# Attention pairs of a fused attention and expert kernel: q and k projected once and doubled by DMA, values one unit later, shared weights rounded behind the first pair

## Chip, cores and metric

One of the eight cores of a Trainium2 chip. The metric is the device time of one execution in microseconds. The engines are TensorE (PE), VectorE (DVE), ScalarE (ACT), GpSimd (POOL) and SyncE (SP); they run their own instruction streams and meet by semaphores. SP, ACT and POOL can issue DMAs.

## What is computed

```python
# B=16, S=128, D=256, 16 heads of 16; then a feed-forward with a shared and 12 routed experts
q = (layernorm(x) @ Wq.T + bq); k = ctx @ Wk.T + bk; v = ctx @ Wv.T + bv     # split into 16 heads
att = einsum('bhsd,bhtd->bhst', q, k) / sqrt(16)
att = where(pad_mask == 0, -1e9, att); att = where(subsq_mask == 0, -1e9, att)
x = x + einsum('bhst,bhtd->bhsd', softmax(att), v)
xf = layernorm(x)
w = top-2 of (xf @ Wr + br) / 1.5, softmax over the two
x = x + geglu(xf @ Ws1 + bs1) @ Ws2 + bs2 + sum over the two experts of w * (geglu(xf @ We1 + be1) @ We2 + be2)
```

## The kernel before

**Pairs and units.** The 16 batches go through the attention in 8 pairs, each pair in four units: batch `b = n // 2` of the pair, half `u = n % 2` of the heads. A unit makes scores of 8 heads in PSUM `ps_s` (`scores`), DVE takes the maximum and subtracts it (`softmax_shift`, L1011 and L1017, into `prob`), ACT takes the exponential (`exp`, L775), PE transposes the probabilities in two halves through the one bank `ps_t[0]` (`prob_transposes`, L493), ACT copies each half to `probT` (`prob_copy`, L766), PE multiplies with the values (`values`, L505), and after two units ACT copies the output to `outT` (`out_copy`, L771) and PE transposes it (`out_transposes`, L514). DVE divides by the sums (`norm`), adds to x and takes the statistics of the second layernorm (`residual`), and after POOL's square root (`rstd`) applies it (`ln2_apply`).

**One unit behind.** In unit U of the loops PE does the scores of U, and then the transposes and values of unit U-1; between them stand the steps of `PLAN`, which project the next pair: transposes of ctx (`cT`) and of the normed x (`xT`), the k projection in two steps (`k0`, `k1`), v, and q in two steps, and for the pair before the router's transposes and logits (`r`, `l`). All is done in about twice f32r precision: ACT rounds to a high part, DVE takes the difference as the low part, and products are made of high and low parts. Each step passes PE, ACT, DVE in turn; `xb_ready`, `xb_hi` and `xb_free` count them, and the steps take turns on two PSUM banks.

**Doubled heads.** A head has 16 numbers, but scores are products over 32 rows: q's high parts stand in 16 rows and its low parts in the other 16, against k twice. So that PSUM holds this layout at once, the weights of q and k come to the chip with each head's columns twice (`heads` in `kernel`), 512 columns instead of 256, in four groups of 128. `q_st` is what the products read, `q_cut` the high part masked to the low rows, `k_hi` and `k_lo` the parts of k.

**What sets the order.** Each engine's function writes its instructions in program order; `pair(p, par, first, last)` is written once per engine, and pairs 1 to 4 run in hardware loops. POOL before the pairs rounds the shared expert's weights (`convert`, six pieces of 512 columns to high and low) and starts the loads of expert 0. In the pairs it only takes square roots. SP loads ctx, and stores the normed x of the pair before (`save_xn2`).

## Time and profile before

| | us |
|---|---|
| median of 3 runs | 782.37 (781.30 to 784.15) |
| profiled execution | 781.65 |
| its span, first to last instruction | 779.5 |
| PE busy in the span | 640.2 (82%) |
| DVE, ACT, POOL busy | 457.8, 270.1, 330.0 |
| mean granted clock of TensorE | 0.926 of full speed |

The profile is of one execution. The span leaves out 2.15 us of the execution's time. A busy matmul is pipelined with its neighbours, so start-to-start distances tell its cost better than its duration. An engine's idle time before an instruction is given in brackets in a timeline, with the one that released it.

### The profile page before, as it was taken

How to read it: one execution, taken by the hardware profiler on the slowest of the kernel's cores; microseconds unless marked ns; L12 is line 12 of the kernel's file. 1: busy time of each engine (PE TensorE's matmuls, PEld its weight loads, DVE VectorE, ACT ScalarE, POOL GpSimd, SP SyncE). 2: the span in 40 equal slices, each digit the busy share in tenths (PEclk: the TensorE clock that was granted, in tenths of full speed). 3: DMA queues.
4: the chain of work that ended last, by engine and by line, in shares of the span. 5: the costliest groups of instructions: out<-in, count | busy, mean ns of one | idle time of the engine just before them, and what ended most of it. 6: DMA issues, size and time to landing. Idle time of an engine off the chain costs nothing.

```text
span 779.5 us, 16006 instructions
## 1 busy us (share of the span) xinstructions
PE 640.2 (82%) x4977; PEld 590.3 (76%) x4978; DVE 457.8 (59%) x893; ACT 270.1 (35%) x556; POOL 330.0 (42%) x389
## 2 busy tenths in 40 slices
PE   4699899899987776079999999999999999997041
PEld 4577777777865665079999999999999999997041
DVE  4656677676765583056665656656566565663136
ACT  3245555555544311024333333333333333331010
POOL 0610000000000477790847957677878582006710
PEclk9689999999999898579999999999999999999556
DMA  9930101001001143252344435525554241013412
GB/s 305 371 133 15 42 28 40 13 27 42 1 29 41 42 148 109 101 189 61 104 162 150 161 119 191 161 76 193 189 177 153 101 135 40 27 40 99 118 48 81
DMA packets 44289, 83.03 MB, mean 107 GB/s; under 512 B 4832, under 2 KB 32736, under 8 KB 44128
## 3 DMA queue, kind: packets, MB, share of 16 engines
q0 software_dynamic: 11120, 48.24, 18.4%
q1 hardware_dynamic: 32560, 34.04, 13.2%
q10 hardware_dynamic: 576, 0.30, 0.2%
q8 instruction: 21, 0.34, 0.2%
q14 instruction: 12, 0.10, 0.0%
HBM read 60.81 MB, written 19.66 MB: 103 GB/s over the span
## 4 chain that ended last, share of the span: by engine, by line
PE 71%; DVE 8%; another core or an unknown queue 8%; issue 5%; ACT 5%; SPq 1%; DMA 1%; POOL 0%; DVEq 0%; ACTq 0%
PE ps_s L583 27%; PE ps_o L623 15%; PE ps_t L596 5%; PE ps_t L493 4%; PE ps_s L481 4%; PE ps_o L505 4%; PE ps_t L440 3%; ACT probT L766 2%; PE ps_x L440 2%; PE ps_s L476 2%; DVE x_all L1264 2%; PE ps_x L605 1%; DMA br<-in_br 1%; DVE ag L1176 1%
## 5 line engine op out<-in xcount | busy, mean ns | idle before, releaser
L583 PE MATMUL ps_s<-ring,xTh 128*128 (+1 forms) x944 | 203.0, 337 | 4.9 <-issue 4.4
L623 PE MATMUL ps_o<-ring,hTh 128*128 (+1 forms) x644 | 127.3, 297 | 65.6 <-DVE hTl L1188 59.0
L583 PEld LDWEIGHTS ps_s<-ring,xTh 128*128 128x128 f32 x944 | 155.3, 193 | 8.3 <-issue 5.4
L623 PEld LDWEIGHTS ps_o<-ring,hTh 128*128 128x128 f32 x644 | 103.1, 198 | 67.4 <-issue 57.3
L1298 POOL TENSOR_TENSOR ring<-stage,ring 128x512 fp32r<-128x512 f32 x120 | 150.9, 1287 | 2.3
L1176 DVE TENSOR_TENSOR ag<-ps_s,up_bias 128x768 f32<-128x768 f32 (+1 forms) x96 | 88.8, 925 | 67.0 <-PE ps_s L583 45.4
L838 ACT ACTIVATE hTh<-ps_t 128x384 fp32r<-128x384 f32 (+1 forms) x118 | 54.6, 462 | 207.1 <-PE ps_t L596 138.9
L583 PE MATMUL ps_s<-ring,xTl 128*128 (+1 forms) x472 | 115.5, 325 | 2.1 <-issue 2.0
L1286 POOL TENSOR_TENSOR ve<-mv,eps 128x2 f32<-128x2 f32 x16 | 3.1, 197 | 232.4 <-DVE mv L1043 170.9
L623 PE MATMUL ps_o<-ring,hTl 128*128 (+1 forms) x322 | 93.3, 290 | 0.0
L831 ACT ACTIVATE ps_s<-ag 128x384 f32<-128x384 f32 (+1 forms) x118 | 55.1, 467 | 90.7 <-DVE ag L1176 85.4
L583 PEld LDWEIGHTS ps_s<-ring,xTl 128*128 128x128 f32 x472 | 83.8, 192 | 0.6 <-issue 0.6
L1182 DVE TENSOR_TENSOR ag<-ag,ps_s 128x384 f32<-128x384 f32 (+1 forms) x118 | 61.1, 518 | 37.6 <-ACT ps_s L831 31.1
L1188 DVE TENSOR_TENSOR hTl<-ps_t,hTh 128x384 fp32r<-128x384 f32 (+1 forms) x118 | 60.9, 517 | 23.6 <-ACT hTh L838 19.1
L1294 POOL TENSOR_SCALAR ring<-stage 128x512 fp32r<-128x512 f32 x120 | 71.7, 626 | 4.8 <-DVE logits L966 4.0
L596 PE MATMUL ps_t<-const,ag 128*128 128x128 f32 x322 | 57.1, 282 | 8.3 <-issue 7.5
L623 PEld LDWEIGHTS ps_o<-ring,hTl 128*128 128x128 f32 x322 | 63.8, 198 | 0.0
L766 ACT ACTIVATE probT<-ps_t 128x512 f32<-128x512 f32 x64 | 38.2, 596 | 69.5 <-PE ps_t L493 69.5
L1409 POOL DMA_INDIRECT gath<-rows_out,idx_top x32 | 30.8, 961 | 67.1 <-DMA rows_out<-y_row 57.6
L1193 DVE TENSOR_TENSOR xTl<-ps_x,xTh 128x256 fp32r<-128x256 f32 x59 | 25.0, 424 | 50.9 <-ACT xTh L845 44.5
L596 PEld LDWEIGHTS ps_t<-const,ag 128*128 128x128 f32 x322 | 38.5, 143 | 15.0 <-issue 10.4
L1011 DVE TENSOR_REDUCE nmax<-ps_s 128x8 f32<-128x1024 f32 x32 | 39.0, 1220 | 16.6 <-PE ps_s L481 16.5
(194 smaller groups left out, 1018.6 us busy)
## 6 DMA issues: line engine op xcount, KB each, us to landing
stage<-in_w POOLq DMA_DIRECT2D x12, 1536.0 KB, 6.7
stage<-in_w POOLq DMA_DIRECT2D x12, 768.0 KB, 5.4
up_bias<-in_bias POOLq DMA_DIRECT2D x12, 768.0 KB, 4.8
rows_in<-y_row SPq DMA_DIRECT2D x1, 5504.0 KB, 22.3
xrow<-rows_in SPq DMA_DIRECT2D x43, 128.0 KB
rows_out<-y_row SPq DMA_DIRECT2D x43, 128.0 KB, 1.7
cbuf<-in_ctx SPq DMA_DIRECT2D x8, 256.0 KB, 3.2
xn_all<-xn2p SPq DMA_DIRECT2D x8, 256.0 KB, 2.4
```

The costliest lines, as they stand in the source:

```text
L583: last = pe_.matmul(out, x[:, c, :], weights(place, a, half_w), start=n == 0, stop=n == 5)
L596: last = pe_.transpose(ps_t[:, u, c * P:(c + 1) * P], ag[u][:, 0, c * P:(c + 1) * P], ident)
L623: pe_.matmul(ps_o[:, 0:D], h[u][:, c, :], weights(place, a, D), start=n == 0, stop=False)
L766: act.activation(probT[:, jj, :, :], ps_t[:, 0, :].rearrange("p (g t) -> p g t", g=4), ACT.Identity).then_inc(pt_copied, 1)
L831: act.activation(ps_s[:, 2 * u + 1, 0:half_w], ag[u][:, 1, 0:half_w], ACT.Gelu).then_inc(gelu_done[u], 1)
L838: act.activation(hTh[u][:, 0:nch, :], ps_t[:, u, 0:nch * P].rearrange("p (c n) -> p c n", c=nch), ACT.Identity).then_inc(ht_hi[u], 1)
L1011: vec.tensor_reduce(nmax[:, :, :], src, AX.X, ALU.max, negate=True).then_inc(maxed, 1)
L1176: vec.tensor_tensor(ag[u][:, :, 0:half_w], ps_s[:, 2 * u:2 * u + 2, 0:half_w], bias, ALU.add)\
L1182: vec.tensor_tensor(ag[u][:, 0, 0:half_w], ag[u][:, 0, 0:half_w], ps_s[:, 2 * u + 1, 0:half_w], ALU.mult)\
L1188: vec.tensor_tensor(hTl[u][:, 0:nch, :], ps_t[:, u, 0:nch * P].rearrange("p (c n) -> p c n", c=nch), hTh[u][:, 0:nch, :].bitcast(f32), ALU ...
L1294: last = pool.tensor_scalar(hi_ap[:, c:c + PIECE], src[:, c:c + PIECE], 1.0, 0.0, ALU.mult, ALU.add)
L1298: last = pool.tensor_tensor(lo_ap[:, c:c + PIECE], src[:, c:c + PIECE], hi_ap[:, c:c + PIECE].bitcast(f32), ALU.subtract)
```

## The change

1. `wq`, `wk` come with their 256 columns once. The q and k projections are one step each (`PLAN`), of two groups of 128 columns. ACT and DVE write high and low parts into `q_cut` and `k_cut`.
2. These are stored to DRAM (`q_dram` by SP, `k_dram` by POOL), and read back so that q's high and low rows interleave (four DMAs of 128 KB on SP, `spread_q`) and each k row stands twice (eight DMAs of 128 KB on POOL, `spread_k`). PE waits for all of them (`k_in`, `q_in`) before the first scores of a pair.
3. `probT` becomes two buffers, and `values` of unit U-2 stand between the two transposes of unit U-1. `out_transposes`, `norm` and `residual` move with them by a unit. ACT's exponential moves ahead of the output copy and the second probability copy.
4. POOL's rounding of the shared weights and the first loads of expert 0 move behind pair 0; in the prologue q comes before v, and DVE's masks behind v's low part.

```diff
-    PLAN = [["cT", "xT", "k0"], ["v", "k1"], ["r", "q0"], ["q1", "l"]]
+    PLAN = [["cT", "xT", "k"], ["q"], ["v"], ["r", "l"]]
@@ sync @@
+            def save_q(pp, idx):
+                sp.wait_ge(xb_free, idx + 1)
+                sp.dma_start(q_dram.rearrange("(a p) n -> p a n", p=P),
+                             q_cut[:, :, :, :].rearrange("p h g n -> p (h g) n").bitcast(f32)).then_inc(q_saved, 16)
+            def spread_q(pp, par):
+                sp.wait_ge(q_saved, pp * 16 + 16)
+                for g in range(4):
+                    sp.dma_start(q_st[par][:, g, :].bitcast(f32),
+                                 q_dram.rearrange("(h r) n -> r h n", h=2)[g * 64:(g + 1) * 64]).then_inc(q_in, 16)
@@ sync @@
             def pair(p, par, first, last):
                 if not last:
                     sp.wait_ge(xb_ready, index_of("cT", p, first, last) + 1)
-                    load_ctx(p + 2)
+                    if not (isinstance(p, int) and p + 2 >= PAIRS):
+                        load_ctx(p + 2)
+                    save_q(p + 1, index_of("q", p, first, last))
                 if not first:
                     save_xn2(p - 1)
+                if not last:
+                    spread_q(p + 1, 1 - par)
@@ tensor, in pair @@
                     if n == 0:
                         pe.wait_ge(xb_free, before(p, 0, 0, first, last))
+                        pe.wait_ge(k_in, p * 128 + 128)
+                        pe.wait_ge(q_in, p * 64 + 64)
                     scores(p, par, n)
...
                     if prev:
-                        prob_transposes(p * 4 + n - 1, pn, 0)
+                        prob_transposes(p * 4 + n - 1, (n - 1) % 4, 0)
                     next_step()
+                    if behind:
+                        values(p * 4 + n - 2, pn, ppar, pbatch)
                     if prev:
-                        prob_transposes(p * 4 + n - 1, pn, 1)
+                        prob_transposes(p * 4 + n - 1, (n - 1) % 4, 1)
                     next_step()
-                    if prev:
-                        values(p * 4 + n - 1, pn, ppar, pbatch)
                     next_step()
-                    if n % 2 == 0 and prev:
+                    if n % 2 == 1 and behind:
                         out_transposes(pbatch)
@@ scalar, in pair @@
                     if prev:
-                        prob_copy(U, 0)
+                        prob_copy(U, (n - 1) % 4, 0)
                     next_step()
+                    exp(p * 4 + n, n)
+                    if n % 2 == 1 and not (first and n < 2):
+                        out_copy(p * 2 + (n - 2) // 2)
                     if prev:
-                        prob_copy(U, 1)
-                    if n == 0:
-                        next_step()
-                    if n % 2 == 0 and prev:
-                        out_copy(p * 2 + (n - 1) // 2)
-                    exp(p * 4 + n, n)
+                        prob_copy(U, (n - 1) % 4, 1)
@@ vector, in pair @@
-                    if n == 3:
-                        residual(p, 0)
-                    if n == 1 and not first:
+                    if n == 0 and not first:
+                        residual(p - 1, 0)
+                    if n == 2 and not first:
                         residual(p - 1, 1)
@@ gpsimd @@
+            def save_k(pp, idx):
+                if not (isinstance(pp, int) and pp == 0):
+                    gp.wait_ge(ticked, pp * 2)
+                gp.wait_ge(xb_free, idx + 1)
+                pool.tensor_tensor(ptick[:, :], half[:, 0:1], half[:, 0:1], ALU.add).then_inc(ticked, 1)
+                gp.dma_start(k_dram.rearrange("(a p) n -> p a n", p=P),
+                             k_cut[:, :, :, :].rearrange("p h g n -> p (h g) n").bitcast(f32)).then_inc(k_saved, 16)
+            def spread_k(pp, par):
+                gp.wait_ge(ticked, pp * 2 + 1)
+                gp.wait_ge(k_saved, pp * 16 + 16)
+                pool.tensor_tensor(ptick[:, :], half[:, 0:1], half[:, 0:1], ALU.add).then_inc(ticked, 1)
+                for hl, t in ((0, k_hi), (1, k_lo)):
+                    for g in range(4):
+                        rows = k_dram[hl * D + g * 64:hl * D + (g + 1) * 64, :]
+                        gp.dma_start(t[par][:, g, :].bitcast(f32), rows.rearrange("(r o) n -> r o n", o=1)
+                                     .broadcast_to([64, 2, 256])).then_inc(k_in, 16)
...
             def pair(p, par, first, last):
+                if not last:
+                    save_k(p + 1, index_of("k", p, first, last))
                 if not first:
                     rstd(ln2_var, ln2_rs, mv2, ve2, rs2, p - 1, pstep2)
+                if not last:
+                    spread_k(p + 1, 1 - par)
                 if not last and not (isinstance(p, int) and p + 2 >= PAIRS):
                     rstd(ln1_var, ln1_rs, mv1, ve1, rs1, p + 2, pstep)
```

POOL in a pair of the loop, before: `ve`, `rs` with 73 and 74 are the square root of the second layernorm, with 69 and 70 that of the first.

```order
L1286 TENSOR_TENSOR ve_73<-mv_72,eps 128x2
L1288 TENSOR_TENSOR rs_74<-ve_73,half 128x2
L1285 REGISTER_ALU
L1286 TENSOR_TENSOR ve_69<-mv_68,eps 128x2
L1288 TENSOR_TENSOR rs_70<-ve_69,half 128x2
```

The same place now:

```order
L1329 TENSOR_TENSOR ptick<-half 128x1
L1330 DMA k_dram<-k_cut 128x4x256
L1307 TENSOR_TENSOR ve_73<-mv_72,eps 128x2
L1309 TENSOR_TENSOR rs_74<-ve_73,half 128x2
L1335 REGISTER_ALU
L1336 ISA
L1337 TENSOR_TENSOR ptick<-half 128x1
L1341 DMA k_hi_114<-k_dram 128x1x256 x4
L1341 DMA k_lo_116<-k_dram 128x1x256 x4
L1306 REGISTER_ALU
L1307 TENSOR_TENSOR ve_69<-mv_68,eps 128x2
L1309 TENSOR_TENSOR rs_70<-ve_69,half 128x2
```

The store of k stands ahead of the second layernorm's square root of the pair before, the eight reads behind it and ahead of the first layernorm's.

ACT in units 0 and 1 of a loop pair, before:

```order
L766 ACTIVATE probT<-ps_t 128x512
L741 REGISTER_ALU
L743 ACTIVATE aTh_106<-ps_t 128x512
L770 ISA
L771 ACTIVATE outT<-ps_o 128x512
L774 REGISTER_ALU
L775 ACTIVATE prob_118<-prob_118 128x1024
L741 REGISTER_ALU
L754 ACTIVATE k_hi_112<-ps_x,bks 128x256 x2
```

And now, from the exponential of unit 0 to k's high part, and the end of unit 1:

```order
L803 ACTIVATE prob_120<-prob_120 128x1024
L791 REGISTER_ALU
L794 ACTIVATE probT_123<-ps_t 128x512
L770 REGISTER_ALU
L772 ACTIVATE aTh_106<-ps_t 128x512
L770 REGISTER_ALU
L777 ISA
L779 ACTIVATE k_cut<-ps_x,bks 128x256 x2
```

```order
L803 ACTIVATE prob_121<-prob_121 128x1024
L798 ISA
L799 ACTIVATE outT<-ps_o 128x512
L791 REGISTER_ALU
L794 ACTIVATE probT_122<-ps_t 128x512
```

The exponential stood behind the second probability copy, x's high part and the output copy; it now stands ahead of all three.

## Rows read from the trace of the kernel before

**Rows 1.** Timeline: first mask products of pairs 0, 1, 3, 7 (start, us, engine, line, operation).
```profile
30.34 1.01 PE L476 MATMUL ps_s<-mask_b,ident_b 128*128 128x512 bf16 x2 [4.34 <-DVE q_st L955]
...
62.34 0.61 PE L476 MATMUL ps_s<-mask_b,ident_b 128*128 x2
...
118.10 0.60 PE L476 MATMUL ps_s<-mask_b,ident_b 128*128 x2 [0.30 <-DVE logits L966]
...
228.79 0.61 PE L476 MATMUL ps_s<-mask_b,ident_b 128*128 128x512 bf16 x2
```

**Rows 2.** Stretches: length, busy PE, PEld, DVE, ACT, POOL (instructions), clock, DMA share, GB/s.
```profile
62.34:228.79 166.45, 153.40 (x1550) 129.49 (x1549) 115.16 (x240) 90.58 (x156) 9.73 (x22) 1.00 0.08 28
...
49.10:53.18 4.08, 2.20 (x27) 1.64 (x25) 1.56 (x6) 2.69 (x5) 0.90 (x2) 0.99 0.01 4
53.40:59.90 6.50, 6.50 (x36) 5.61 (x35) 4.67 (x9) 0.85 (x3) 0.00 (x0) 0.50 0.00 0
```

**Rows 3.** PE's waits in 62.34 to 228.79: total us, times, longest.
```profile
PE ps_o L514 <- ACT outT L771: 4.4, 6, 0.7
PE ps_t L493 <- ACT probT L766: 4.0, 12, 0.3
```

**Rows 4.** Timeline of the loop pair that begins at 118.10.
```profile
119.78 1.22 DVE L1011 TENSOR_REDUCE nmax<-ps_s 128x8 f32<-128x1024 f32 x1 [1.29 <-PE ps_s L481]
...
120.44 0.60 ACT L766 ACTIVATE probT<-ps_t 128x512 f32<-128x512 f32 x1 [2.82 <-PE ps_t L493]
...
122.16 1.22 DVE L1017 TENSOR_TENSOR prob<-ps_s,nmax 128x1024 f32<-128x1024 f32 x1
...
124.06 1.05 ACT L775 ACTIVATE prob<-prob 128x1024 f32<-128x1024 f32 x1
...
125.17 0.84 ACT L754 ACTIVATE k_hi<-ps_x,bks 128x256 fp32r<-128x256 f32 x2
...
129.94 0.41 DVE L1035 TENSOR_TENSOR x_all<-x_all,att 128x256 f32 x1
...
131.46 0.69 POOL L1288 TENSOR_TENSOR rs<-ve,half 128x2 f32<-128x2 f32 x1
...
141.34 0.48 PE L440 MATMUL ps_t<-aTh,wqh 128*128 128x256 f32 x2
...
142.85 0.60 PE L493 MATMUL ps_t<-const,prob 128*128 128x128 f32 x4
```

**Rows 5.** Timeline of POOL: issues of DMAs.
```profile
330.11 0.96 POOL L1376 DMA_INDIRECT rows_in<-xn_all,idx_top  x1 [0.30 <-issue]
331.07 1.17 POOL L1336 DMA_DIRECT2D up_bias<-in_bias  x2
...
350.45 0.92 POOL L1318 DMA_DIRECT2D stage<-in_w  x1 [0.30 <-POOL ring L1298]
```

**Rows 6.** DMA issues by line: count, KB each, median us from issue to landing.
```profile
stage<-in_w POOLq DMA_DIRECT2D x12, 1536.0 KB, 6.7
...
rows_out<-y_row SPq DMA_DIRECT2D x43, 128.0 KB, 1.7
...
wk_raw<-in_wk SPq DMA_DIRECT2D x1, 512.0 KB, 5.6
...
up_bias<-in_bias POOLq DMA_DIRECT2D x1, 512.0 KB, 4.2
```

**Rows 7.** Timeline of DVE in the prologue.
```profile
13.73 0.88 DVE L958 SCALAR_TENSOR_TENSOR k_lo<-ps_x,bks,k_hi 128x256 fp32r<-128x256 f32 x2 [3.44 <-ACT k_hi L754]
...
18.46 1.23 DVE L985 TENSOR_SCALAR keep<-pad_b 128x2048 f32<-128x2048 int32 x1 [1.98 <-DMA br<-in_br]
...
22.19 1.23 DVE L993 TENSOR_SCALAR mask_b<-keep 128x2048 bf16<-128x2048 f32 x1
```

**Rows 8.** Timeline of PE behind the last pair.
```profile
252.63 0.66 PE L493 MATMUL ps_t<-const,prob 128*128 128x128 f32 x4
...
257.92 0.60 PE L514 MATMUL ps_o<-const,outT 128*128 128x128 f32 x4
```

More of the change, by code:

```diff
@@ L39 @@
 C_ID, C_UP = 0, P
-C_LOQ = 2 * P
-C_LOB = C_LOQ + 1
+C_LOB = 2 * P
 C_ROW = C_LOB + 1
@@ L142, in build @@
     aTl = [put(f"aTl{i}", [P, KC, 256], f32r, low) for i in range(2)]
+    k_cut = put("k_cut", [P, 2, 2, 256], f32r, low)
+    q_cut = put("q_cut", [P, 2, 2, 256], f32r, low)
     q_st = [put(f"q_st{i}", [P, 4, 256], f32r, low) for i in range(2)]
@@ L277, in before @@
     def before(p, n, k, first, last):
-        base = len(PROJ) if first else 9 * p + 5
+        base = len(PROJ) if first else PAIR_STEPS * p + len(PROJ) - 2
         return base + sum(len(steps(m, first, last)) for m in range(n)) + k
@@ L327, in load_ctx @@
                              .rearrange("(t p) d -> p t d", p=P)).then_inc(ctx_in, 16)
+            def save_q(pp, idx):
[7 more added lines that the diff above has]
+                                 q_dram.rearrange("(h r) n -> r h n", h=2)[g * 64:(g + 1) * 64]).then_inc(q_in, 16)
             sp.wait_ge(xb_ready, PROJ.index("cT") + 1)
             load_ctx(1)
+            save_q(0, PROJ.index("q"))
+            spread_q(0, 0)
             sp.wait_ge(w_ready, 3)
@@ L369, in _ @@
             pair(PAIRS - 3, 1, False, False)
-            save_xn2(PAIRS - 3)
+            pair(PAIRS - 2, 0, False, False)
             save_xn2(PAIRS - 2)
@@ L455, in router @@
             def router(s, q, idx, bank):
-                pe.wait_ge(xb_free, idx - (0 if isinstance(idx, int) and idx == PAIR_STEPS_END + 1 else 1))
+                pe.wait_ge(xb_free, idx - (1 if s == "r" else 0))
                 ps = step_bank[bank]
@@ L540, in pair @@
                     prev = not (first and n == 0)
-                    pn, ppar, pbatch = (n - 1) % 4, par if n else 1 - par, p * 2 + (n - 1) // 2
+                    behind = not (first and n < 2)
+                    pn, ppar, pbatch = (n - 2) % 4, par if n >= 2 else 1 - par, p * 2 + (n - 2) // 2
                     def next_step():
@@ L674, in _ @@
             x_transposes(0, 0, 0)
+            values(UNITS - 2, 2, 1, B - 1)
             prob_transposes(UNITS - 1, 3, 1)
-            values(UNITS - 1, 3, 1, B - 1)
             pe.wait_ge(converted, 1)
@@ L679, in _ @@
             up(0, 0, 0, False, SH)
+            values(UNITS - 1, 3, 1, B - 1)
+            up(0, 0, 1, False, SH)
             out_transposes(B - 1)
-            up(0, 0, 1, False, SH)
             router("r", PAIRS - 1, PAIR_STEPS_END, 0)
@@ L757, in step @@
                     sc.wait_ge(xb_free, idx)
+                    if not (isinstance(pp, int) and pp < 2):
+                        sc.wait_ge(pv_done, pp * 8 - 8)
                     act.activation(v_sb[par][:, :, :, 0:HD],
@@ L1068, in pair @@
                     softmax_shift(p * 4 + n, n, next_step if n == 0 and todo else None)
-                    if n == 3:
-                        residual(p, 0)
-                    if n == 1 and not first:
+                    further = not last and not (isinstance(p, int) and p + 2 >= PAIRS)
+                    if n == 0 and not first:
+                        residual(p - 1, 0)
+                    if n == 2 and not first:
                         residual(p - 1, 1)
-                    further = not last and not (isinstance(p, int) and p + 2 >= PAIRS)
-                    if n == 1 and not first:
-                        ln2_apply(p - 1)
                     if n == 2 and further:
                         ln1_stats(p + 2)
-                    if n == 2:
-                        norm(p, 0)
                     while todo:
                         next_step()
-                    if n == 0 and not first:
+                    if n == 2 and not first:
+                        ln2_apply(p - 1)
+                    if n == 3:
+                        norm(p, 0)
+                    if n == 1 and not first:
                         norm(p - 1, 1)
@@ L1221, in tile @@
                     y_copy(t - 1, s - 1 if prev_s is None else prev_s, prev_routed, par, turn)
+            residual(PAIRS - 1, 0)
             x_lo(0)
@@ L1302, in _ @@
             gp.wait_ge(setup_ready, 1)
+            def save_k(pp, idx):
+                if not (isinstance(pp, int) and pp == 0):
+                    gp.wait_ge(ticked, pp * 2)
[12 more added lines that the diff above has]
+                                     .broadcast_to([64, 2, 256])).then_inc(k_in, 16)
             rstd(ln1_var, ln1_rs, mv1, ve1, rs1, 0, pstep)
+            save_k(0, PROJ.index("k"))
+            spread_k(0, 0)
             rstd(ln1_var, ln1_rs, mv1, ve1, rs1, 1, pstep)
-            gp.wait_ge(shared_in, 32)
             SH, PIECE = RING - 1, 512
-            convert(stage1[:, 0:W1S], ring[:, SH, 0:W1S], ring[:, SH, W1S:2 * W1S], 1)
-            convert(stage2[:, 0:W2S], ring[:, SH, 2 * W1S:2 * W1S + W2S],
-                    ring[:, SH, 2 * W1S + W2S:2 * W1S + 2 * W2S], 2).then_inc(converted, 1)
             def load_raw1(e):
```

132 lines of the change are left out of this document (68 added, 64 removed).

## The prediction

> **What bounds the kernel now.** I read the timeline of TensorE (PE) first. It cuts the profiled execution (span 779.5 us, 781.65 us with the 2.15 us around it, 0.7 us under the median of 782.37) into a prologue up to 30.34, attention pair 0 up to 62.34, pairs 1 to 6 up to 228.79, and the last pair up to about 252.6 [rows 1]. Everything behind (feed-forward) is unchanged, and its first steps hang on the last pair, so attention time passes to the end one for one. The change touches only what lies before 262.
>
> In pairs 1 to 6 a pair takes 166.45 / 6 = 27.74 us, PE is busy 153.40 of 166.45 us and its granted clock is 1.00 [rows 2]. The other 13.05 us, 2.2 per pair, are short waits, most of them for ScalarE (ACT): 4.4 us for its copy of the output, 4.0 for its copy of the transposed probabilities [rows 3]. So PE's own work bounds these pairs, 25.6 us each.
>
> **What leaves PE.** A projection step of twelve products of 128x256 takes 141.34 to 142.85, 1.51 us [rows 4]. There are four for q and k per pair, two stay: 3.0 us less. DVE and ACT each lose four of their eight operations for q and k. With the values one unit later, PE no longer waits for the second probability copy. PE's work falls to 25.6 - 3.0 = 22.6 us. If this alone counted, six pairs would give back up to 6 x (27.74 - 22.6) = 31 us. I do not believe it, because of two orders.
>
> **The order inside a pair.** I lay one new pair from its first mask product (0), with durations and gaps of rows. Scores take PE to 1.57; DVE's maximum starts at 1.68 (119.78 against 118.10), the shift at 4.06 and ends at 5.28 (122.16 + 1.22), in a pair whose cT low half sits between, as here [rows 1, 4]. The exponential of 1.05 ends at 6.4 [rows 4], and ACT's order now is exponential, second probability copy, xT high half, k high half (0.6, 0.6, 0.84): k's high half ends at 8.1. DVE's k low half (0.88, [rows 7]) ends at 9.0. Only then is DVE free for the maximum of unit 1, whose scores PE had ready at 7.6. Its shift ends at 11.5, exponential at 12.6, output copy (now behind the exponential) at 13.1: PE, which has run out of work at 11.1, waits 2.0 us for it and starts unit 2 at 13.6. There the shift ends at 17.8 and residual(p-1, 1) starts; its x_all row to the end of the POOL square root is 129.94 to 131.46 + 0.69, 2.2 us [rows 4], so ln2's rs is there at 20.0. Unit 3 waits 1.1 us for the output copy in the same way and ends at 25.5. So with all data at hand a pair is 25.5, not 22.6.
>
> **The order on POOL, where the change hangs.** The eight DMAs that spread k for the next pair stand on POOL behind rstd(ln2, p-1), and so behind the residual in unit 2. They start at 20.1. PE waits for them before the first scores of the next pair (k_in). Two plain issues in a row take 1.17 us, 0.59 each, for 128 rows; one of 768 rows takes 0.92; an indirect one of 128 rows 0.96 + 0.30 [rows 5]. I take 0.59, the row with as many rows and no index list; 0.9 and 1.26 stay as bounds. The last is issued at 20.1 + 7 x 0.59 = 24.3. Landing: a POOL load of 1536 KB takes 6.7 us from its issue and one of 512 KB 4.2 [rows 6], 2.5 us per MB, so 128 KB take about 3.3; a 128 KB store of SP lands in 1.7, the low bound. The last lands at 27.6, PE's next pair begins at about 28.0 with 0.3 to 0.4 for the 2 MB (k 1, q 0.5, xn2 0.5) that share this stretch. q on SP waits for save_xn2(p-1) likewise: xn2 is ready at 20.9, two saves, four issues of 0.5, so it lands near 26.3, behind k's cover. **Bound without a clock effect: 28.0 per pair, +0.3.**
>
> The Trainium skill's page DMA: Bandwidth & Descriptors (Anatomy of one DMA, SWDGE path) gives 2.0 us fixed plus bytes at 436 GB/s for a DMA from POOL; that would be an estimate of 2.3 us for 128 KB. By it a pair would be 1.0 us shorter and the sum 6 us less. The rows of this case speak against it: 512 KB would be 3.2 by the page and took 4.2 [rows 6].
>
> **The clock.** In that order PE idles from 24.0 to 25.1, transposes for 0.45, and idles again from 25.5 to 28.0: busy 0.45 of 4 us. In pair 0 of the trace PE is busy 2.20 of 4.08 us in 49.10 to 53.18, and the clock then stands at 0.50 of its full 2.4 GHz, 1.2 GHz, for the 6.50 us from 53.40 [rows 2]. So I expect a fall at each pair's start. Cold, unit 0's scores take 2.9 instead of 1.57, transposes 0.8 for 0.5; moved through the chain above, k's high half waits for a k step that ends 2.6 later, of which 0.7 lies in slack: k low half at 10.9 instead of 9.0. Everything behind, the residual in unit 2 and the spread too, moves by 1.9. **A pair takes 28.0 + 1.9 = 29.9 us, +2.16 each, +13.0 for six.** If PE falls a second time in the 2.0 us wait of unit 1, the scores of unit 2 come 1.3 later, 31.2.
>
> **Prologue.** Before, DVE ends k's low half at 14.6 and builds the masks from 18.46 (released by the br load) to 23.4 [rows 7]; PE's first scores wait to 30.34 for the last q half [rows 1]. After, weights are half as wide, but POOL does save_k (0.9 + about 3.5 landing), eight issues (4.7), and only then rstd(ln1, 1), for which DVE waits before wvl and the masks: k low half 13.9, saved 18.5, issued 23.8, ln1 rs 24.8, xn 25.6, wvl 26.3, masks of 5.0 us to 31.3. First scores at 31.4: +1.1; if the save lands as slowly as the wk load of 512 KB did (5.6, [rows 6]), +3.
>
> **Pair 0.** It was 32.0 us. Two k and q steps go, one of them at the low clock (2.7), and units 0 and 1 have less to wait for. Laid out as above it ends at 24.6; but k of pair 1 is saved and spread beside the rows_in zeroing and the shared weights, which now start after spread_q, so I take the landing, 26. That is -6.0, between -4 and -7. The shared conversion moves behind it on POOL: its cover is 13 us between ln1 of pair 2 and the k save of pair 2, nothing else waits; without that cover save_k(2) would slip us for us.
>
> **Last pair and tail.** The last pair has no projections; exponentials and output copies bound it: about 21.7, 22.7 with a low clock at its start, against 252.63 - 228.79 = 23.8: -1.1. In the tail the output transposes stood 5.3 us behind the last probability transposes [rows 8]; now values of unit 30 (1.0) fill a wait and the second half of the first up product (1.5) stands before them, less what the output copy had waited: +1.0.
>
> **Sum.** +1.1 - 6.0 - 1.1 + 1.0 = -5.0, and +13.0 of six pairs: +8.0. 781.65 + 8.0 = **789.6 us**. Each 1 us of the period counts 6.
>
> **The rivals.** (A) No fall of the clock: 28.0 per pair, -5.0 + 1.6 = -3.4, 778.2. For it: in the last pair PE waits often and keeps its clock; against it, 53.40 [rows 2]. (B) The spread is not late: landing as on SP (1.7) gives about 26.3, the engines' own bound 25.5: -5.0 - 8.6 to -13.4, 768 to 763. It needs issues and landings both at their low ends. (C) Slower still, by one mechanism: POOL's issue of a k spread costs more than 0.59. At 0.9 it adds 7 x 0.31 = 2.2 per pair, 13 in all, 803; at 1.26, 28 in all, 818. The sum is above zero from a period of 27.74 + 5.0 / 6 = 28.6 on, which is an issue cost of 0.40 if the clock falls and of 0.67 if not. A second fall of the clock works the same way, 31.2 or 797.
>
> The Trainium skill's page SBUF — State Buffer (SBUF: two separate sides) speaks for (C): while VectorE runs an operation in a 2-port mode, GpSimd cannot write the descriptors of its DMAs. Here ln2_apply lies on the issues; as a mechanism of this kernel it could cost at most that operation's 0.74 us per pair, 4.4 us. No row here shows it.
>
> **How the numbers follow.** Forecast 0.38 (own range 783 to 794), A 0.20 (774 to 782), B 0.14, C with the second fall 0.28. A measurement can tell about 0.5%, 3.9 us. Slower by more: C and 0.32 of the forecast, 0.60. Within: 0.06 of the forecast and 0.11 of A, 0.17. Faster: 0.09 of A and B, 0.23. The range 770 to 806 leaves out most of B (0.12) and the far end of C (0.08).
>
> **What would show it.** Right: PE's largest wait is the first mask product on the k spread, 2 to 4 us, seven times; the clock at half speed in the first 6 us of pairs; starts of pairs 29 to 31 us apart; POOL's issues beginning about 20 us into a pair, each near 0.6. Wrong: no such wait (B), a clock of 1.00 throughout (A), issues of 0.9 and more (C), or a DVE order that lets unit 1 start its maximum at 7.7.

## Result and profile of the changed kernel

The changed kernel takes 807.1 us (median of 4 runs, 805.6 to 809.2) against 783.3 for the kernel before in the same job, a ratio of 1.033 with an interval of 1.028 to 1.038 (ratios in this document are the record's for fast runs, and the plain quotient of the two medians, here 1.030, can differ by some thousandths). It is slower, as forecast, but by 24 us and not by 8: the time lies just above the range (770 to 806). Its profiled execution has a span of 806.3 us (808.16 with what lies around it), the one of before 779.5, so 26.8 us are to be explained; the forecast had 8.0.

TensorE's timeline, first mask product of each pair from pair 0 on (column 1 the start, in brackets how long PE idled ahead of it and for what), answers to [rows 1]; the last three lines are units 1, 2 and 3 of the last pair:

```profile
31.72 1.03 PE L501 MATMUL ps_s<-mask_b,ident_b 128*128 128x512 bf16 x2 [1.51 <-DVE mask_b L1013]
...
60.00 1.03 PE L501 MATMUL ps_s<-mask_b,ident_b 128*128 x2 [1.04 <-DMA q_st<-q_dram]
...
91.43 1.03 PE L501 MATMUL ps_s<-mask_b,ident_b 128*128 x2 [3.75 <-DMA q_st<-q_dram]
...
122.67 1.03 PE L501 MATMUL ps_s<-mask_b,ident_b 128*128 x2 [3.50 <-DMA q_st<-q_dram]
...
251.04 1.01 PE L501 MATMUL ps_s<-mask_b,ident_b 128*128 128x512 bf16 x2 [4.43 <-DMA q_st<-q_dram]
257.68 0.65 PE L501 MATMUL ps_s<-mask_b,ident_b 128*128 128x512 bf16 x2
264.02 0.59 PE L501 MATMUL ps_s<-mask_b,ident_b 128*128 128x512 bf16 x2
270.22 1.06 PE L501 MATMUL ps_s<-mask_b,ident_b 128*128 128x512 bf16 x2
```

The first product is at 31.72 (before 30.34). Pair 0 takes 28.28 us (32.00). Pairs 1 to 6 take (251.04 - 60.00) / 6 = 31.84 (27.74), and behind the last pair's start come 555.3 us (550.7). That is +1.4, -3.7, +24.6 and +4.6, together +26.8 before rounding. The waits of PE from 30 to 260 answer to [rows 3] (total, times, longest):

```profile
PE ps_s L501 <- DMA q_st<-q_dram: 24.6, 7, 4.4
PE ps_o L539 <- ACT outT L799: 13.1, 13, 2.0
PE ps_s L501 <- DVE mask_b L1013: 1.5, 1, 1.5
```

PE waits at every pair's start, and what comes last is q's spread on SP, not k's on POOL. Pair 1 (it began at 60.00) shows why; first POOL's timeline, then SP's DMA queue (start, duration, xcount of issues):

```profile
81.05 0.19 POOL L1307 TENSOR_TENSOR ve<-mv,eps 128x2 f32<-128x2 f32 x1 [9.02 <-DVE mv L1063]
81.33 0.71 POOL L1309 TENSOR_TENSOR rs<-ve,half 128x2 f32<-128x2 f32 x1
82.02 0.18 POOL L1337 TENSOR_TENSOR ptick<-half 128x1 f32<-128x1 f32 x1
82.15 2.45 POOL L1341 DMA_DIRECT2D k_hi<-k_dram x4
84.34 2.70 POOL L1341 DMA_DIRECT2D k_lo<-k_dram x4
```

```profile
83.05 0.56 SPq L368 DMA_DIRECT2D xn_all<-xn2p x1
83.82 0.58 SPq L369 DMA_DIRECT2D xn_dram<-xn2p x1
84.54 3.10 SPq L345 DMA_DIRECT2D q_st<-q_dram x4
```

k is asked for from 22.15 us into the pair on, q from 24.54 on, each behind the work of ln2 (the second layernorm of the pair before). Both bursts and the two stores of xn2 then share the DMA engines. The landings (KB each, median us from issue to landing, over 60 to 250) are:

```profile
k_hi<-k_dram POOLq DMA_DIRECT2D x24, 128.0 KB, 3.1
k_lo<-k_dram POOLq DMA_DIRECT2D x24, 128.0 KB, 4.6
q_st<-q_dram SPq DMA_DIRECT2D x24, 128.0 KB, 4.6
...
xn_dram<-xn2p SPq DMA_DIRECT2D x6, 256.0 KB, 4.8
```

and the windows of the same stretch (length, busy time of PE, PEld, DVE, ACT, POOL, then granted clock, DMA share, GB/s) show full DMA engines, an idle PE, and then a PE at half clock (0.50 of full speed, 1.2 GHz):

```profile
84.00:88.00 4.00, 2.72 (x30) 2.19 (x24) 1.70 (x4) 2.37 (x4) 3.92 (x7) 1.00 0.96 306
88.00:91.00 3.00, 0.00 (x0) 0.00 (x0) 1.07 (x3) 0.00 (x0) 0.06 (x1) 0.92 0.76 251
91.00:97.00 6.00, 5.57 (x34) 4.21 (x36) 1.30 (x2) 1.20 (x2) 0.00 (x0) 0.50 0.01 3
```

### The profile page after: what moved, and what is told of

The parts are those of the page before. It is cut to its first block, busy times and chain, and to the rows that moved or that the text cites. A ratio compares the mean times of both kernels' runs of the same rounds, so it can differ in the third digit from the quotient of the medians.

```text
span 806.3 us, 15708 instructions
## 1 busy us (share of the span) xinstructions
PE 648.8 (80%) x4785; PEld 590.8 (73%) x4786; DVE 448.1 (56%) x860; ACT 254.3 (32%) x524; POOL 378.9 (47%) x477
## 4 chain that ended last, share of the span: by engine, by line
PE 62%; DVE 10%; another core or an unknown queue 8%; issue 7%; DMA 6%; SPq 2%; ACT 2%; POOL 2%; DVEq 0%; ACTq 0%; POOLq 0%
PE ps_s L611 28%; PE ps_o L651 14%; PE ps_t L624 5%; DMA q_st<-q_dram 4%; PE ps_s L506 4%; PE ps_t L518 2%; PE ps_s L501 2%; DVE nmax L1031 2%; DVE x_all L1285 2%; SPq L345 2%; DVE prob L1037 2%; PE ps_x L633 2%; PE ps_o L530 1%; PE ps_x L465 1%
## 5 line engine op out<-in xcount | busy, mean ns | idle before, releaser
L611 PE MATMUL ps_s<-ring,xTh 128*128 (+1 forms) x944 | 206.5, 341 | 19.5 <-issue 15.5
L611 PEld LDWEIGHTS ps_s<-ring,xTh 128*128 128x128 f32 x944 | 158.2, 197 | 22.7 <-issue 16.0
L651 PE MATMUL ps_o<-ring,hTh 128*128 (+1 forms) x644 | 127.1, 297 | 38.4 <-DVE hTl L1208 30.4
L1202 DVE TENSOR_TENSOR ag<-ag,ps_s 128x384 f32<-128x384 f32 (+1 forms) x118 | 61.1, 518 | 37.6 <-ACT ps_s L856 30.7
L1307 POOL TENSOR_TENSOR ve<-mv,eps 128x2 f32<-128x2 f32 x16 | 7.5, 466 | 97.0 <-DVE mv L1063 92.2
## 6 DMA issues: line engine op xcount, KB each, us to landing
rows_in<-y_row SPq DMA_DIRECT2D x1, 5504.0 KB, 23.7
```

What stands on the lines that cost most here:

```text
L611: last = pe_.matmul(out, x[:, c, :], weights(place, a, half_w), start=n == 0, stop=n == 5)
L651: pe_.matmul(ps_o[:, 0:D], h[u][:, c, :], weights(place, a, D), start=n == 0, stop=False)
L1202: vec.tensor_tensor(ag[u][:, 0, 0:half_w], ag[u][:, 0, 0:half_w], ps_s[:, 2 * u + 1, 0:half_w], ALU.mult)\
```

## Experiments

The kernel before took 782.3, 784.0 and 728.2 us in the three jobs of these runs. The third is a case of its own (last section), and only ratios are compared across jobs. What can be compared directly is the start of the last pair in the profiled execution: behind it come 547.6 to 550.9 us where that pair runs at full clock and 553.1 to 557.5 where it begins at half clock or waits, in the first two jobs; in the third 497.1 and 497.6 in the two kernels without a wait there. The last column is the mean length of the pairs named in brackets, those in which a kernel has settled.

| kernel | ratio to before [interval] | start of last pair | mean pair (which pairs) |
|---|---|---|---|
| before | 1 | 228.79 | 27.7 (3 to 6) |
| changed | 1.033 [1.028, 1.038] | 251.04 | 31.8 (1 to 6) |
| e1_spread_first | 0.996 [0.992, 1.000] | 223.62 | 25.5 (3 to 6) |
| e2_keep_warm | 1.021 [1.014, 1.027] | 243.46 | 30.3 (1 to 6) |
| e3_q_stays | 1.026 [1.020, 1.032] | 242.60 | 30.4 (1 to 6) |
| e4_values_later_alone | 0.996 [0.992, 1.000] | 229.02 | 27.5 (3 to 6) |
| e5_spread_first_early_weights | 1.000 [0.996, 1.004] | 228.93 | 25.4 (4 to 6) |
| e6_out_copy_ahead_of_exp | 0.978 [0.969, 0.987] | 219.58 | 23.5 (2 to 4) |
| e8_k_spread_first_alone | 1.014 [1.005, 1.024] | 238.16 | 28.8 (2 to 6) |
| e9_q_spread_first_alone | 1.021 [1.011, 1.031] | 243.92 | 30.7 (1 to 6) |
| e7_early_weights_alone | 1.049 [1.040, 1.058] | 263.24 | 32.0 (2 to 6) |
| e11_zero_rows_later | 1.031 [1.022, 1.040] | 246.13 | 31.8 (2 to 6) |
| e10_loads_behind_first_pair | 0.969 [0.961, 0.978] | 212.86 | 23.5 (3 to 6) |
| e12_expert_load_behind_pair_1 | 0.967 [0.958, 0.976] | 208.50 | 23.7 (5 and 6) |

### Both spreads first on their queues

```diff
 # GpSimd, pair()
+                if not last:
+                    spread_k(p + 1, 1 - par)
                 if not first:
                     rstd(ln2_var, ln2_rs, mv2, ve2, rs2, p - 1, pstep2)
-                if not last:
-                    spread_k(p + 1, 1 - par)
 # SyncE, pair()
+                if not last:
+                    spread_q(p + 1, 1 - par)
                 if not first:
                     save_xn2(p - 1)
-                if not last:
-                    spread_q(p + 1, 1 - par)
```

> The changed kernel, with only the place of the spreads changed: on POOL spread_k stands ahead of the second layernorm's square root, on SP spread_q ahead of save_xn2. Theory (the spreads are late because they stand behind the residual of unit 2, and the clock falls in the wait they make): no wait on k_in or q_in at the pairs' starts, clock 1.00 in pairs 1 to 6, a pair takes the 25.5 us of the engines' chain instead of 31.8, total near 768. Rival (2.5 MB per pair through DRAM cannot be had in time whatever the order): the wait at the first mask product stays over 2 us and the total over 790. Second rival (the values one unit later are what costs): pairs stay above 29 us without a wait on the spreads.

Pairs 1 to 6 take 33.75, 28.02, 25.52, 25.45, 25.00 and 25.97 us. From pair 3 on they have the length that the prediction laid out for "all data at hand", 25.5, with no wait for either spread and a granted clock of 0.98 over the four pairs; waits for the output copy remain, about two per pair (16.0 us in 13 waits, 2.0 at most). So queue order accounts for the whole of the steady loss, 31.8 against 25.5. The second rival, that the later values are what costs, is out with it. The run came to 779 us and not to the expected 768: the gain is eaten in pairs 1 and 2, and POOL's timeline of pair 1 says by what:

```profile
68.47 0.81 POOL L1352 DMA_DIRECT2D stage<-in_w  x1 [0.30 <-POOL ring L1319]
69.28 0.86 POOL L1356 DMA_DIRECT2D stage<-in_w  x1
...
71.15 0.79 POOL L1330 DMA_DIRECT2D k_dram<-k_cut  x1
80.26 0.19 POOL L1337 TENSOR_TENSOR ptick<-half 128x1 f32<-128x1 f32 x1 [8.32 <-DMA k_dram<-k_cut]
80.39 2.45 POOL L1341 DMA_DIRECT2D k_hi<-k_dram  x4
```

Expert 0's 2.25 MB are issued just ahead of k's save, for which POOL then waits 8.3 us (2.7 in the pairs behind); with the new order ln2's square root stands behind that, and PE waits 4.3 us for xn2p, around which its granted clock goes from 1.00 (78 to 81) to 0.50 (90 to 96). The issues cost 0.61 each here, with no ln2_apply beside them, and as much in the changed kernel, where ln2_apply (82.17 to 82.9) lies on the first four.

### One queue at a time

e8_k_spread_first_alone makes only POOL's half of that edit, e9_q_spread_first_alone only SP's.

> The changed kernel with POOL's order alone changed: k's eight copies ahead of rstd(ln2); q's four stay behind save_xn2 on SP. Theory (both queues were late and their copies shared the DMA engines with each other and with xn2): k lands near 20 us into the pair, q is asked for at 24.5 as before, and with half of the burst gone it lands in 2.9 us instead of 4.5, so the next pair starts 1.5 to 2 us earlier, 29.5 to 30.5 us periods, the only long wait is q_st with 1.5 to 2.5 us, the clock still falls in most pairs: 795 to 800 us. Rival (POOL's order was the whole cause, q is covered): periods 25.5 to 26, 780 us. Other rival (SP's order was the whole cause): nothing changes, 807 us.

> The changed kernel with SP's order alone changed: q's four copies ahead of save_xn2; k's eight stay behind rstd(ln2) on POOL. Theory (both were late, k a little less): k is asked for at 22.2 to 26.9 us into the pair and its last copy lands in 2.9 to 3.3 us instead of 4.5, so the next pair starts at 29.5 to 30.5, waiting on k_lo for 2 to 2.5 us, the clock still falls: 795 to 802 us. Rival (SP's order and q alone held the pairs back): periods 25.5 to 26, 780 us.

With k first, pairs 2 to 6 take 28.8 us, a little less than expected, and end in a wait of 1.3 to 1.8 for q; pair 1 takes 34.6, for k's save stands behind expert 0's loads there as in e1_spread_first. With q first pairs take 30.7 and end in a wait of 2.0 to 2.8 (put down to k_lo in the first three, in the others to issue, which means that the profile shows no releaser). At the 782.4 us of before these ratios are 793.5 and 799: both rivals that made one queue the whole cause (780) are out, and so is "nothing changes". The landings over 120 to 250, of k first:

```profile
k_lo<-k_dram POOLq DMA_DIRECT2D x16, 128.0 KB, 3.2
q_st<-q_dram SPq DMA_DIRECT2D x16, 128.0 KB, 2.7
```

and of q first:

```profile
q_st<-q_dram SPq DMA_DIRECT2D x16, 128.0 KB, 2.6
k_hi<-k_dram POOLq DMA_DIRECT2D x16, 128.0 KB, 3.2
k_lo<-k_dram POOLq DMA_DIRECT2D x16, 128.0 KB, 4.0
```

q's copies land in 2.6 to 2.7 us when k's are not beside them and in 4.6 in the changed kernel; k_lo in 3.2 alone, in 4.0 with only the stores of xn2 beside it (q first), and in 4.6 with both. In e1_spread_first, where the two spreads overlap and xn2's stores come later, both land in 3.9 (121 to 223). So the crowd adds 1.4 to 1.9 us to a landing, and xn2's stores are part of it.

### Keeping PE busy through the wait

```diff
+                        if not (isinstance(p, int) and p == 0):
+                            for _w in range(17):
+                                pe_.matmul(ps_x[:, :].rearrange("p (g t) -> p g t", g=4), ident_b[:, :],
+                                           mask_b[:, 0:1, :].broadcast_to([P, 4, P]), start=True, stop=True)
                         pe.wait_ge(k_in, p * 128 + 128)
```

> The changed kernel with 17 products of 128x512 into a free PSUM bank ahead of the wait for the spreads at the start of pairs 1 to 7; their result is never read. Theory (the fall of the clock is a cost of its own, 1.9 us per pair): the clock stays at 1.00, the wait for the spreads shrinks by what the products take, the pairs fall from 31.8 to about 29.8, total near 794. Rival (the low clock only fills slack, the period is set by the transfers alone): the clock stays up and the total stays at 807.

In five of the seven starts the clock is now full; this kernel's window around its start at 182.34:

```profile
178.00:182.00 4.00, 3.83 (x20) 2.05 (x21) 1.33 (x4) 0.61 (x2) 0.00 (x0) 1.00 0.47 169
182.00:188.00 6.00, 6.00 (x63) 4.91 (x62) 3.47 (x6) 1.52 (x3) 0.00 (x0) 1.00 0.15 46
```

At the last two starts it still falls (0.75 over 213 to 217, 0.73 over 243 to 249), and at two others no wait is left, so the dummy products may have held PE up themselves. Pairs take 30.3 us instead of 31.8. The clock at half speed behind the wait is thus worth at least 1.5 us of a pair, near the 1.9 of the prediction; the 4.8 us between 30.3 and 25.5 are for the most part the data's lateness, which dummy work does not touch.

### q's spread taken away in pairs 1 to 6

```diff
-                if not last:
+                if first:
                     spread_q(p + 1, 1 - par)
...
-                        pe.wait_ge(q_in, p * 64 + 64)
+                        pe.wait_ge(q_in, 64 if first else 128)
```

> The changed kernel without the read-back of q from pair 2 on: pairs 2 to 7 compute with the q of pairs 0 and 1, all else is as it was, so the output is not the reference's. It takes 512 KB of about 2 MB out of the stretch of transfers in units 2 and 3. Theory (the stretch is bound by the 16 DMA engines together, at about 330 GB/s): the wait stays but is now for k, which lands 1.5 us sooner, pairs near 30.3, total near 798. Rival (only q's queue on SP is late, k is there in time): the wait falls to under 1.5 us and the pairs to 28 or less, total under 785.

Pairs take 30.4 us and end in a wait of 1.8 to 3.4, now for k_lo or for what the trace calls issue; k_lo lands in 4.0 us instead of 4.6. So q, with its lateness on top of k's and its share of the crowd, costs 1.4 us per pair, and k alone, with the fallen clock, the other 4.9 above 25.5.

### The values one unit later, alone

The kernel before with part 3 only: two probT buffers, the values of unit n-2 in unit n, and the plan `[["cT","xT","k0"],["v","k1"],["q0","q1"],["r","l"]]`; q and k are projected twice as before.

> The kernel before with part 3 of the change alone: two probT buffers, values of unit U-2 between the transposes of unit U-1, output transposes, norm, residual and ACT's order as in the changed kernel; q and k are still projected twice as wide, without any DMA (steps: cT xT k0 | v k1 | q0 q1 | r l), and the shared weights are rounded in the prologue. Theory: PE's work stays at 25.6 us per pair, the waits for ACT's copies shrink but the output transposes wait 1 to 2 us behind the exponential, so pairs of 26 to 28 against 27.7 and a total of 775 to 785. Rival (the new order of ACT costs more than it saves): pairs above 28.5 and a total above 788.

0.996: the steady pairs take 27.5 us (27.7 before) and wait 6.0 us for the output copy between 58 and 235. Pair 0 takes 27.9 instead of 32.0, but pair 1 31.5 instead of 27.9, at a granted clock of 0.54 in its first 10 us, and pair 2 29.2. This part alone neither costs nor brings anything that a measurement tells apart with certainty; what [rows 3] had shown as waits on the probability copy is all but gone (0.6 us), and nearly as much stands elsewhere.

### Where the shared weights are rounded

e5_spread_first_early_weights is e1_spread_first with `shared_weights()` moved back ahead of `pair(0, ...)` on POOL; e7_early_weights_alone makes that one move in the changed kernel.

> Both spreads first on their queues, as in e1_spread_first, and part 4 undone: POOL rounds the shared weights ahead of the first pair, as in the kernel before, and expert 0's 2.25 MB are asked for there. In e1_spread_first pairs 1 and 2 took 33.75 and 28.02 us and the later ones 25.0 to 26.0, and in pair 1 k's save stood behind the rounding (56.86 to 68.2) and behind those 2.25 MB, landed after 8.3 us, and with it rstd(ln2) and the r transposes came late. Theory: the rounding's new place is the whole cause, so pairs 1 and 2 come to 25.5 to 26 as well and the first pair stays at 28 to 29: 779.4 - 8 - 2.5 = 769 us (764 to 773), no wait on xn2p or q_st in pair 1. Rival: the shared weights hold up the first pair instead (k's first save and spread are then queued on POOL ahead of the rounding, but the 2.25 MB still fall into the first pair beside the 5.5 MB that SP writes to rows_in), pair 0 goes to 32 as in the kernel before and the gain is 4 to 6 us.

> The changed kernel with part 4 alone undone: shared weights rounded ahead of the first pair, and expert 0's 2.25 MB asked for there, ahead of k's save for pair 1 on POOL's queue. Theory, from e5_spread_first_early_weights (its k save landed at 59.8, and pair 1 began 37.2 us after pair 0 where e1_spread_first took 28.5): part 4 spares the first pair that wait and is the one part that helps, so the first pair grows by 7 to 9 us, pairs 1 to 6 stay 31 to 32.5 apart, and the run is 812 to 818 us. Rival: the rounding in pair 1 costs there as much as it spares (pair 1 gets shorter by as much as pair 0 gets longer), 804 to 810 us.

e5_spread_first_early_weights brought nothing (1.000). The rival named the right place, the first pair, but not the size: it expected 32 us there and a small gain. The longest of PE's waits from 58 to 250 is now

```profile
PE ps_s L501 <- DMA k_lo<-k_dram: 13.3, 1, 13.3
```

Pair 0 takes 37.16 us (28.46 in e1_spread_first). k's save for pair 1 now has to wait for the rounding on POOL (it is issued at 46.34 and POOL goes on behind it at 59.77), and lands behind expert 0's 2.25 MB and beside the 5.5 MB of zeros. Alone in the changed kernel (e7) the same move puts the last pair's start 12.2 us later (263.24 against 251.04): pair 0 takes 38.2, pair 1 33.8. POOL's timeline shows both halves of the cost, first in e7, then in the changed kernel:

```profile
48.80 0.79 POOL L1330 DMA_DIRECT2D k_dram<-k_cut  x1
61.71 0.19 POOL L1337 TENSOR_TENSOR ptick<-half 128x1 f32<-128x1 f32 x1 [12.12 <-DMA k_dram<-k_cut]
```

```profile
42.42 0.81 POOL L1330 DMA_DIRECT2D k_dram<-k_cut  x1 [0.25 <-issue]
50.63 0.18 POOL L1337 TENSOR_TENSOR ptick<-half 128x1 f32<-128x1 f32 x1 [7.40 <-DMA k_dram<-k_cut]
```

The save is asked for 6.4 us later, because POOL rounds until 46.7 and then issues the two loads, and it takes 12.9 us instead of 8.2 from its issue until POOL goes on. So of the four parts of the change, this one gave 12 us, and the prediction gave it no term in its sum.

### The zeros out of the first pair

e11_zero_rows_later: SP issues the zeroing of rows_in behind `pair(0, ...)` instead of ahead of it.

> The changed kernel with SP's 5.5 MB of zeros to rows_in asked for behind the first pair's work on SP instead of ahead of it. In the changed kernel k's save for pair 1 took from 42.4 to 50.6 to land beside these 5.5 MB, SP stood 10.9 us at cbuf's load, and pair 1's start waited 1.04 us for q_st. Theory of the crowded first pair: with the zeros gone k lands early and pair 1 starts 1.0 to 1.5 us sooner, the first pair takes 27 us instead of 28.3, the zeros then lie beside pair 1's own saves, where they cost little: 804 to 807 us. Rival: the first pair's length is its own 8 us at half clock at the start (unit 0 took 8.1 us) and ACT's and DVE's work, not the zeros: within 0.5 us for pair 0, and pair 1 gets longer by 2 us or more because its saves are now late: 808 to 812 us.

```profile
31.08 0.60 PE L501 MATMUL ps_s<-mask_b,ident_b 128*128 128x512 bf16 x2 [1.58 <-DVE mask_b L1013]
...
54.93 0.60 PE L501 MATMUL ps_s<-mask_b,ident_b 128*128 x2
...
87.39 1.03 PE L501 MATMUL ps_s<-mask_b,ident_b 128*128 x2 [6.11 <-DMA k_lo<-k_dram]
```

Pair 0 takes 23.85 us, 4.4 less than with the zeros and a far larger gain than I expected. The windows of the changed kernel and of this one tell that it is not the wait at the end alone:

```profile
30.00:38.00 8.00, 5.93 (x31) 4.37 (x31) 4.49 (x5) 1.20 (x2) 0.00 (x0) 0.50 0.97 355
38.00:46.00 8.00, 8.00 (x43) 6.95 (x43) 4.20 (x6) 2.98 (x5) 1.01 (x2) 0.50 1.09 385
```

```profile
30.00:38.00 8.00, 6.36 (x39) 5.37 (x40) 4.20 (x5) 2.28 (x4) 0.00 (x0) 0.67 0.57 205
38.00:46.00 8.00, 7.45 (x68) 6.00 (x68) 6.45 (x9) 4.26 (x8) 2.72 (x6) 0.91 0.30 106
```

The granted clock is 0.50 over all 16 us in the one and 0.67 and 0.91 in the other. That difference is not the zeros' doing. The same windows of e9_q_spread_first_alone, which has the zeros in pair 0, and of e10_loads_behind_first_pair, which has them behind it, are the other way round:

```profile
30.00:38.00 8.00, 5.78 (x57) 4.51 (x57) 4.64 (x5) 2.97 (x6) 0.00 (x0) 1.00 1.01 344
38.00:46.00 8.00, 6.69 (x56) 6.15 (x55) 7.54 (x14) 3.86 (x7) 1.01 (x2) 0.88 1.08 391
```

```profile
30.00:38.00 8.00, 6.28 (x32) 4.92 (x33) 4.15 (x4) 1.23 (x3) 4.18 (x6) 0.50 0.57 201
38.00:46.00 8.00, 8.00 (x44) 6.95 (x44) 4.02 (x5) 2.75 (x6) 7.80 (x9) 0.52 0.00 0
```

The clock of the first pair's first half differs from kernel to kernel, and no run shows what decides it. What the zeros do is hold the data: with them pair 0 takes 28.1 to 28.5 us in the changed kernel, e1, e3, e8 and e9, and its last 1.0 to 4.0 us are a wait for q, longest in e9, whose units are fast. Without them the clock decides, though e10 and e12 also have the edit on ScalarE of the next section: 23.85 (e11) and 23.89 (e12) at the higher clocks, 27.45 in e10 at half clock, of which 2.00 is a wait for k_lo, whose save stands behind the rounding there. At the clock that the changed kernel had, I estimate from this that the zeros cost it little more than its wait of 1.04 us, and my expected 27 was about right for that case. The zeros then lie on pair 1 together with expert 0's loads; its k save takes 14.2 us to land, and the pair behind it starts after 6.1 us of waiting for k_lo. In all the last pair starts 4.9 us earlier; by the ratios the gain is 1.4 us, well within their intervals, so the run times do not show it.

### Putting it together

e6_out_copy_ahead_of_exp is e5_spread_first_early_weights with one more edit on ScalarE:

```diff
+                    if n % 2 == 1 and not (first and n < 2):
+                        out_copy(p * 2 + (n - 2) // 2)
                     exp(p * 4 + n, n)
-                    if n % 2 == 1 and not (first and n < 2):
-                        out_copy(p * 2 + (n - 2) // 2)
```

> e5_spread_first_early_weights with one more edit: in units 1 and 3 ACT copies the outputs (outT) ahead of the exponentials. In e1_spread_first PE waited 16.0 us in 13 waits on outT, at most 2.0 each, two per pair. Theory: the values are done before the scores are shifted, so the copy costs the exponentials 0.3 to 0.5 us at most and these waits go: a pair gives 1.0 to 2.0 us, seven pairs 7 to 14, so 756 to 762 us. Rival: the copy waits for the values, ACT holds the exponentials back by as much as PE won, PE then waits for prob transposes' copies: within 2 us of e5_spread_first_early_weights.

The waits for outT (14.5 us in e5) do not show any more, and pairs 2 to 4 take 23.7, 23.6 and 23.2 us where e5's steady pairs take 25.4: 0.978, 2.2% below e5. The prediction's 2.0 us wait in unit 1 was therefore real, and the order of two lines caused it. Pairs 5 and 6 take 26.0 and 26.7 again. The granted clock is 0.50 from 190 to 199 there, behind no longer wait of PE than 0.88 us; no run shows why.

e10_loads_behind_first_pair adds to that the zeros behind `pair(0, ...)` on SP and expert 0's loads behind it on POOL. e12_expert_load_behind_pair_1 keeps the rounding behind the first pair as in the changed kernel, and asks for expert 0's weights behind pair 1.

> e6_out_copy_ahead_of_exp with the two large transfers out of the first pair: the zeros to rows_in (SP) and expert 0's load (POOL) are asked for behind the first pair's save and spread; the rounding of the shared weights stays ahead of it. Theory: pair 1 of e6_out_copy_ahead_of_exp waited 15.9 us for k_lo only because k's save was queued beside these, so the first pair falls from 37.8 to 26 or 27 us and the run from 765.7 to 754 to 758 us. Rival: k's save in pair 1 then comes beside the 7.75 MB instead (23 us of transfer at the 340 to 390 GB/s seen) and pair 2's start waits 5 us or more: 760 to 765 us.

> e1_spread_first with ACT's output copy ahead of the exponentials, the zeros to rows_in behind the first pair and expert 0's load behind pair 1's save and spread (POOL rounds the shared weights behind the first pair, as in the changed kernel). Theory: no k save then stands behind a large transfer; the first pair takes 27 to 28 us, pair 1 25 (its k save waits for the end of the rounding, 68 us, and the zeros), pair 2 24 to 25, later pairs 23.5: 752 to 757 us. Rival: POOL's rounding beside pair 1 slows DVE and holds k's save past its need, pair 1 takes 30 us or more: 759 to 763 us.

At 782.4 us these ratios would be 758 and 756.5; the third job lacks some 50 us outside attention (last section), so this makes a gain in attention look larger than it is, and by the last pair's start the gains are 15.9 and 20.3 us. In the first, pair 0 takes 27.45 and pair 1, which has the 7.75 MB, 33.0. In the second pair 1 takes 31.4 where I expected 25: the rival, that the rounding in pair 1 holds k's save past its need, came true in that pair (POOL goes on behind that save at 74.0, 8.5 us after its issue). The pairs take 23.89, 31.4, 24.4, 24.3, 25.5, 23.7 and 23.7, and of PE's waits from 58 to 250 none is for q or k:

```profile
PE ps_t L442 <- DVE xn2p L1071: 7.8, 3, 5.9
PE ps_x L442 <- DVE xn2p L1071: 7.5, 5, 3.9
```

What is late is ln2 of the pair before, which in this order stands behind the spreads. The two cannot be told apart by their ratios; both are faster than either given kernel, by about 3% against before and, by the ratios of two jobs, 6% against the changed one.

## Why the prediction was off

**The queue order was right.** The prediction put the start of k's issues at 20.1, or 22.0 with a fallen clock; in pair 1 it is 22.15. It put 0.59 on an issue; it is 0.61. ln2's square root was to end at 21.9 (20.0 + 1.9); it ends at 82.04, 22.0. Unit 2 was to start at 15.5 by the same sum; it starts at 15.6. The rival with dearer issues is out. By the Trainium skill (SBUF — State Buffer, SBUF: two separate sides) ln2_apply could have held back POOL's descriptors, if it runs in a 2-port mode. Four issues take 2.45 us with it beside them and 2.45 without (e1), so no run here shows that.

**The failed step is the landing, and with it "q lands near 26.3, behind k's cover".** The prediction gave one copy 3.3 us and the whole burst 0.3 to 0.4 on top, and let q arrive at 26.3 (28.2 with the clock), with the next pair's start at 29.9 for k's sake. It named k's spread as what PE would wait for; PE waits for q, which is there at 31.4, 3.2 later than laid out. Of these, q's issues began 0.7 later (24.5 instead of 23.8) and took 2.6 us instead of 2.0 (3.1 in pair 1), and the remaining 1.4 to 1.9 are the landing. Away from the other queue's copies a copy lands in 3.1 to 3.2 (POOL) or 2.6 to 2.7 (SP). In the burst the last ones, k_lo and q, take 4.6, at a DMA share of 0.96, and e8 and e9 show that this is the crowd. The mean wait at the end of pairs 1 to 6 is 3.9 us where 2.5 was forecast: 8.6 of the 11.6 us by which six pairs missed (24.6 against 13.0). The other 3.0 are not told apart. By the Trainium skill (DMA: Bandwidth & Descriptors, Anatomy of one DMA, SWDGE path) 2.3 us would have been my estimate for one copy from POOL; the traces have more even where it is alone.

**The clock** fell as forecast, at each start (0.50 over the first 6 us of each of pairs 1 to 7), and is worth at least 1.5 us per pair (e2) where I had 1.9.

**Pair 0** gave 3.7 us and not 6.0. I took 26 us for it with a late landing; it is 28.3. The zeros of rows_in are issued at 28.3 now (17.8 before) and land 23.7 us later, inside it, and they hold the data for pair 1 until about 28.2 (e9). This mechanism was named and its size taken too small. The half clock over the pair's first 16 us, which alone would have left about 27.2 (28.28 less the wait of 1.04), stands in the layout of 24.6 nowhere.

**The last pair** was forecast at 1.1 us less. Up to the first half of the last unit's transposes, the end that the prediction used, it took 26.1 us instead of 22.7 (before 23.8); the lines of the changed kernel that answer to [rows 8] are

```profile
277.15 0.63 PE L518 MATMUL ps_t<-const,prob 128*128 128x128 f32 x4
...
283.68 0.60 PE L539 MATMUL ps_o<-const,outT 128*128 128x128 f32 x4
```

The pair began after a wait of 4.43 us, at half clock, and ran at 0.50 again in 266 to 270, with its units 6.6, 6.3 and 6.2 us apart. e1_spread_first, whose last pair begins without a wait, keeps 1.00 throughout, has units of 3.6, 6.3 and 3.6 and takes 21.6 us to the same place, where the forecast had 21.7 for a full clock. So the layout was right, and the 1 us allowed for the clock was not: it cost 4.5. Two falls in one pair were a rival for pairs 1 to 6, and I had not carried it to the pair without projections. In the tail the output transposes stand 6.5 us behind that point instead of 5.3, +1.2, and the transposes of the last xn2p 11.1 instead of 10.0, so +1.0 was right. The other 1.3 of the +4.6 lie in the feed-forward part, whose instructions did not change; what they are is open.

**Prologue** +1.4 against +1.1: right, and PE's last wait there is for the masks (1.51 us), as forecast.

**Part 4** has no term of its own in the sum and spares 12 us in this change (e7): ahead of pair 0 the rounding holds POOL past the moment when k could be saved, and the 2.25 MB that follow it are queued ahead of the save. I had written down its arithmetic and not its loads. It did not enter the error of the sum, as pair 0 was laid out with both behind it, but once the spreads stand first pair 1 pays for the loads (e1, 33.75).

In sum: +0.3 prologue, +2.3 pair 0, +11.6 six pairs, +4.7 last pair and what follows, 18.8 us above the 8.0 before rounding. The direction came out for the reason that was given, and not by luck; the size did not.

## To carry to other kernels

A round trip through DRAM that the next stage waits for belongs ahead of everything on its queues that hangs on late work, and also ahead of large loads that nobody waits for: here the first was worth 6 us of each pair, the second, together with rounding work that held the issuing engine, 12 us once. Lay out each queue of a burst to its last issue, add the landing that copies have in a crowd (here 4.4 to 4.6 us, not the 2.6 to 3.2 of a copy with its queue alone), and ask which queue ends last. Here a PE that idled 3.5 to 4.4 us at a pair's start paid a second time in its clock, at least 1.5 us in pairs with projections and 4.5 in the one without.

## What the runs showed that I had not expected

Between jobs, the same kernel before took 782 to 784 us and then 728 (7 runs, 727.1 to 736.8). In the kernels traced in the third job the pairs have their usual lengths, and what lies behind the last pair is about 50 us shorter (497.1 to 503.4 against 547.6 to 557.5). So the difference stands in the feed-forward part, and there in waits for which the profile names nothing in the core. In the profile of before, taken in the first job, the waits of DVE from 230 to 440 begin with

```profile
DVE ag L1176 <- remote: 20.8, 1, 20.8
```

and over the whole execution its ACT has

```profile
ACT hTh L838 <- remote: 66.5, 4, 22.1
```

In e7, e10, e11 and e12, the four kernels of the third job, no wait on remote is left in any engine's list; the other profiles all have them. What it is, the traces do not say. It seems to hit the kernels of one job alike, which is why ratios within a job are used and absolute times across jobs are not.

An issue can hold SP for long behind a large transfer: the load of cbuf behind the zeros took 10.9 us of SP's time in the changed kernel (11.5 in e5, 13.7 in e9), where the same load takes 0.4 elsewhere.

The granted clock in a profile has to be held against durations. In e2_keep_warm it reads 1.00 over 30 to 38, while the first mask products there take 1.03 us, as they do at 0.50 in the changed kernel, and 0.60 at full clock.
